# The skip product of a graph layer moved from the projection into the aggregation

## What is computed

```
for l in range(2):
    q, k, v = x @ Wq[l] + bq[l], x @ Wk[l] + bk[l], x @ Wv[l] + bv[l]   # 8 heads of 64
    a = (q[dst] * k[src]).sum(-1) * scale                              # scores, per edge and head
    alpha = softmax of a over the edges of each dst
    agg = segment_sum(alpha * v[src], dst)
    x = agg + (x @ Ws[l] + bs[l]) + enc                                # the skip product: x @ Ws[l]
```

## Time and profile before

| | us |
|---|---|
| median of 3 runs (3148.83 to 3156.06) | 3154.48 |
| the profiled execution | 3161.87 |
| its span, the time base of all rows | 3160.2 |

### The profile page before, as it was taken

One profiled execution on the slowest core, in us unless ns is written; L12 is line 12 of the kernel. 1 busy time (PEld: TensorE's weight loads), 2 busy tenths in 40 slices (PEclk: granted clock), 3 DMA queues, 4 the chain that ended last, 5 costly groups with the idle time before them and its releaser, 6 DMA issues. The chain is left out here.

```text
span 3160.2 us, 50179 instructions
## 1 busy us (share of the span) xinstructions
PE 2531.4 (80%) x9914; PEld 1849.9 (59%) x9914; DVE 2163.0 (68%) x3476; ACT 1170.8 (37%) x4350; POOL 1648.5 (52%) x1559
## 2 busy tenths in 40 slices
PE   1888787765898779977877669888785999699998
PEld 1666444443775557744544358666564767477776
DVE  5776677878977666657877888677464454566665
ACT  0554566654000021136666610001353322155554
POOL 0111677777777741146767777777122443355555
PEclk8999788986899989988888779999887999899999
DMA  2666777776777776667777767777432332251110
GB/s 96 237 239 213 246 240 242 240 236 197 204 218 220 218 236 228 197 216 238 240 242 239 221 185 214 213 224 221 150 134 93 106 121 93 98 167 41 40 46 33
DMA packets 244253, 575.14 MB, mean 182 GB/s; under 512 B 32642, under 2 KB 70894, under 8 KB 242834
## 3 DMA queue, kind: packets, MB, share of 16 engines
q0 software_dynamic: 100160, 328.28, 35.8%
q1 hardware_dynamic: 126546, 212.27, 19.7%
q10 hardware_dynamic: 17280, 31.63, 2.7%
HBM read 465.00 MB, written 107.06 MB: 181 GB/s over the span
## 5 line engine op out<-in xcount | busy, mean ns | idle before, releaser
L1357 POOL DMA_INDIRECT edge_ring<-k_rows,edges_src x626 | 592.7, 947 | 282.3 <-issue 135.9
L1357 POOL DMA_INDIRECT edge_ring<-v_rows,edges_src x626 | 617.2, 986 | 223.5 <-issue 140.6
L1666 PE MATMUL edge_psA<-layer_q_space 128*128 128x256 f32 (+1 forms) x2656 | 628.9, 392 | 95.3 <-DVE layer_q_space L1490 87.8
L1666 PEld LDWEIGHTS edge_psA<-layer_q_space 128*128 128x128 f32 x2656 | 495.5, 192 | 228.4 <-issue 159.2
L1490 DVE TENSOR_TENSOR layer_q_space<-edge_ring,edge_psQ 128x512 f32<-128x512 f32 x664 | 426.6, 683 | 162.1 <-SPq L1275 133.1
L1413 DVE TENSOR_TENSOR edge_ring<-edge_psQ,edge_ring 128x512 f32<-128x512 f32 x532 | 346.9, 682 | 175.5 <-ACT edge_ring L1502 71.6
L1502 ACT ACTIVATE edge_ring<-edge_ring 128x64 f32<-128x64 f32 x1328 | 320.1, 242 | 285.9 <-DVE edge_ring L1413 285.9
L1619 PE MATMUL edge_psQ<-layer_q_space,edge_hotT 128*128 x1064 | 363.3, 474 | 15.9 <-DVE edge_ring L1413 13.3
L108 PE MATMUL proj_psP<-proj_w,proj_xT 128*128 128x512 f32 x1440 | 354.9, 403 | 6.5 <-DVE proj_xT L866 4.0
L108 PEld LDWEIGHTS proj_psP<-proj_w,proj_xT 128*128 128x128 f32 x1440 | 270.8, 191 | 68.8 <-DVE proj_xT L866 4.4
L1394 DVE TENSOR_REDUCE layer_scores<-edge_ring 128x24 f32<-128x1536 f32 x166 | 289.1, 1742 | 0.0
(11 more groups left out here) (309 smaller groups left out, 3625.8 us busy)
## 6 DMA issues: line engine op xcount, KB each, us to landing
v_xT<-proj_xT SPq DMA_DIRECT2D x40, 512.0 KB, 4.9
edge_x_halves<-v_xT SPq DMA_DIRECT2D x80, 256.0 KB, 5.4
agg_rows<-layer_q_space ACTq DMA_DIRECT2D x40, 260.0 KB, 3.6
base_rows<-proj_enc SPq DMA_DIRECT2D x40, 256.0 KB, 2.0
k_rows<-proj_out ACTq DMA_DIRECT2D x40, 256.0 KB, 3.8
v_rows<-edge_ring ACTq DMA_DIRECT2D x40, 256.0 KB
edge_ring<-k_rows,edges_src POOLq DMA_INDIRECT x626, 4.0
edge_ring<-v_rows,edges_src POOLq DMA_INDIRECT x626, 3.8
```

The source lines that it names most:

```text
L1357: pool.indirect_dma_start(ring[:, buffer[n], :], None, rows, bass.IndirectOffsetOnAxis(ap=T["src"][:, t:t + 1], axis=0)).then_inc(landed[b ...
L1666: last = pe.matmul(psA[:, bass.ds(d % 2, 1), e, 0:hi - lo].rearrange("p o w -> p (o w)"), hot[:, s % R, :], wv[:, s % R, lo:hi], start=Fal ...
```

## The change

- **The skip product leaves the projection.** `normalise_project` and `combine_project` make K and Q alone (order K, Q, then S and V among the weights), 24 matmuls a tile. The residual that is stored has the skip bias but not the product. Half of the weights' parts are made before the first tile, the other half two at a time in tiles 0 to 3, and at tile 4 SP stores both V's and the skip's parts (2 MB each).
- **It comes back in the aggregation.** SP loads the skip's parts once, behind the masks, then the halves of x a second time, and the residual rows tile by tile. PE makes one chunk (three matmuls) at the start of a batch, four batches for a tile, from batch 2 on (`project_skip`). DVE adds the sum to the residual some batches later (`add_skip`), and SP stores it back.
- **Scores.** ACT makes the one-hots of a batch before it reduces the slot of two batches ago. GpSimd itself tells of landed gathers, four gathers later. SP keeps releases, rows and halves, sorted by slots.
- **First projection.** Four x buffers instead of three, the norm's statistics a tile ahead of its use, units sized and signed one by one, ACT's taking and DVE's rest ahead of DVE's Q addition, PE's unit transposes behind both products.

The core of the diff (`normalise_project` first; `combine_project` has the same edits for `range(2)`, `w_high`, `w_low`, `biased` and the two stores):

```diff
-        layer, XB = 0, 3
+        layer, XB = 0, 4
...
-        S_, K_, Q_, V_ = range(4)
+        K_, Q_, S_, V_ = range(4)
...
-                    if i == 1:
+                    if i == KC:
                         sp.wait_ge(w_lows, 4 * KC)
-                        sp.dma_start(later_v["w"].rearrange("p (h k c) -> p h k c", h=2, k=KC),
-                                     w[:, :, V_ * KC:(V_ + 1) * KC, :].bitcast(F32)).then_inc(v_parts_out, 16)
+                        for name, j in (("w", V_), ("skip_w", S_)):
+                            sp.dma_start(later_v[name].rearrange("p (h k c) -> p h k c", h=2, k=KC),
+                                         w[:, :, j * KC:(j + 1) * KC, :].bitcast(F32)).then_inc(v_parts_out, 16)
...
-                    sp.wait_ge(ready, i * 3 + S_ + 1)
+                    sp.wait_ge(biased, i + 1)
                     sp.dma_start(base_dram[i * P:(i + 1) * P, :], enc[:, i % 2, :]).then_inc(base_out[i % 2], 16)
...
-                    for j in range(3):
+                    for j in range(2):
...
                 for i in range(NT):
                     if i + 1 < NT:
                         high(i + 1)
+                    if i < KC:
+                        w_high(2 * KC + 2 * i)
+                        w_high(2 * KC + 2 * i + 1)
+                    for u in units(i):
+                        size(u)
+                        sign(u)
                     if i:
                         q_part(i - 1)
-                    if i + 2 < NT:
-                        ln.root(act, i + 2)
-                    for u in units(i):
-                        size(u)
                     for u in units(i - 1):
                         take(u)
-                    act.wait_ge(ready, i * 3 + K_ + 1)
+                    if i + 3 < NT:
+                        root(i + 3)
+                    act.wait_ge(ready, i * 2 + K_ + 1)
                     act.dma_start(k_dram[i * P:(i + 1) * P, :], out[:, i % 2, :]).then_inc(k_out[i % 2], 16)
-                    for u in units(i):
-                        sign(u)
...
                     if i + 2 < NT:
-                        normalise(i + 2)
-                    if i:
-                        q_less(i - 1)
-                    add(i, S_)
+                        apply(i + 2)
+                    if i + 3 < NT:
+                        stats(i + 3)
                     add(i, K_)
                     for u in units(i):
                         size_up(u)
-                    for u in units(i):
                         choose(u)
-                    add(i, Q_)
+                    if i:
+                        q_less(i - 1)
                     for u in units(i - 1):
                         low_unit(u)
+                    add(i, Q_)
```

In `edge_attention`, SP, GpSimd, DVE, ACT and PE in turn:

```diff
+                in_turn = [(r + 16, release, (r, multiplied)) for r in range(ET - 3)]
+                for k in range(2, -(-USED // PER_ROWS)):
+                    in_turn.append((k * PER_ROWS - 12, load_rows, (k,)))
+                for h in range(XH, 2 * NT):
+                    in_turn.append((done_in(h - XH) * B, load_half, (h,)))
+                for _slot, do, what in sorted(in_turn, key=lambda x: x[0]):
+                    do(*what)
                 sp.wait_ge(queried, USED)
                 sp.dma_start(masks, T["mask_rows"]).then_inc(masks_in, 16)
+                sp.dma_start(skip_rows[:, 1:, :], later_v["skip_w"].rearrange("p (n c) -> p n c", c=C)
+                             ).then_inc(skip_in, 16)
...
-                for t in range(ET):
-                    if t + AHEAD < ET:
-                        release(t + AHEAD - NV, weighted)
-                    arrive(ET + t, v_arrived)
+                in_turn = [(r + 10, release, (r, weighted)) for r in range(ET - NV)]
+                for h in range(XH, 2 * NT):
+                    i, half = divmod(h - XH, 2)
+                    in_turn.append(((S_AT[i] + 1 + 2 * half) * B, load_half, (2 * NT + h,)))
+                for i in range(NT):
+                    in_turn.append(((S_AT[i] + 7) * B + 1, store_base, (i,)))
+                    if i + 2 < NT:
+                        in_turn.append(((S_AT[i] + 9) * B, load_base, (i + 2,)))
...
+                def arrive(n):
+
+                    pool.wait_ge(*landing[n])
+                    pool.sem_inc(k_arrived if n < ET else v_arrived, 1)
...
                 for t in range(ET):
+                    if t >= FLIGHT:
+                        arrive(t - FLIGHT)
                     if t >= NB:
 
 
                         pool.wait_ge(k_released, t - NB + 1)
-                        pool.sem_inc(started, 1)
                     gather(t, k_dram, t)
...
+                def add_skip(i):
+                    vec.wait_ge(base_in[i % 2], i // 2 * 16 + 16)
+                    vec.wait_ge(s_projected, 4 * i + 4)
+                    vec.tensor_tensor(base_rows[:, i % 2, :], psS[i % 2], base_rows[:, i % 2, :], ALU.add
+                                      ).then_inc(s_added, 1)
...
-                    if j >= 2:
-                        reduce(j - 2)
                     act.wait_ge(spread, j + 1)
...
                     act.activation(hotT[j % 2], apart[:, j % 2, :], ACT.Relu, bias=1.0, scale=-1.0
                                    ).then_inc(hotT_ready, 1)
+                    if j >= 2:
+                        reduce(j - 2)
...
+                def project_skip(i, k):
...
+                    product(pe, psS[i % 2], [x_halves[:, h % XH, part, k % 2, :] for part in range(2)],
+                            [skip_row(part * KC + k) for part in range(2)], start=(k == 0), stop=(k == KC - 1)
+                            ).then_inc(s_projected, 1)
...
                 for s in range(USED):
+                    if s % B == 0 and s // B in s_steps:
+                        project_skip(*s_steps[s // B])
```

More of the change, by code:

```diff
@@ L775, in _ @@
                         for k in range(KC):
-                            last = product(pe, psP[(3 * i + j) % 4][:], [xT[:, i % 2, h, k, :] for h in range(2)],
+                            last = product(pe, psP[(2 * i + j) % 4][:], [xT[:, i % 2, h, k, :] for h in range(2)],
                                            [w[:, h, j * KC + k, :] for h in range(2)],
@@ L905, in _ @@
                                       ALU.subtract).then_inc(w_lows, 1)
+                for i in range(2 * KC):
+                    w_low(i)
                     if i == KC - 1:
@@ L1128, in _, with w_low @@
                 combine_tile(1)
-                for i in range(4 * KC):
+                def w_low(i):
                     vec.wait_ge(w_highs, i + 1)
```

226 lines of the change are left out of this document (138 added, 88 removed).

## The result

The changed kernel takes **3234.26 us** (median of 4 runs, 3233.13 to 3239.1) against 3153.72 for the kernel before on the same chip: a ratio of 1.026, with a 95% interval of 1.0243 to 1.0278. It is slower, by 81 us, where 85 us of gain had been forecast, and the time lies outside the range of 3020 to 3125.

The account below looks back on a forecast made before the run. GpSimd's gathers were taken to bound both edge stages, PE the second projection, unit work the first. Edges -7.5 a layer (-15 for two), projections -46 and -24: -85 us, to 3070 us; range 3020 to 3125.

Parts of the forecast that it names:

- Second projection: PE, near full there, loses 12 of 36 product matmuls a tile: gain of 46 us, bounds 35 to 54.
- First projection: Unit work, not PE, sets the pace; gain of 24 us, 6 in tiles with units and reload, bounds 0 to 45.
- The loop of 11.0 us a tile: First projection: ACT's unit work, SP's store and reload and the landing sum to 11.0 us a tile, against 11.3 before.
- The rival of a longer loop: First projection: the reload loop gets longer, gain -8 instead of -24, total 3086; chance 0.2.
- Scores, -15 a layer: K gathers: stalls and 18 us of release waits go, 3 given back to transfers; bounds -18 and 0.
- SP's release waits: GpSimd's waits read as SP's releases: 18 us in K, 9 in V a layer, both forecast to go.
- near 719: Scores: sign that the last K gather would start near 719 us, with PE's and GpSimd's named waits gone.
- Arrivals told by GpSimd four gathers later and a last store add 1.5: Aggregation: GpSimd's later telling of landed gathers, with a last store, costs 1.5 us a layer.
- must land within four issues, 5.0, so it has 1.2 in hand: Aggregation: a gather lands after 3.8 us and has 5.0, so a margin of 1.2 us.
- Added transfers, +12: Aggregation: added loads and stores slow gathers to a pace of 1.295 us, +12 a layer; bounds 0 to 45.
- The slower one: Aggregation: late gathers, four in flight, carry 1.55 us each, 80 a layer, total 3206; break-even pace 1.45; chance 0.06.
- the +3 forecast: Between scores and aggregation: SP's load of 2 MB skip weights costs V gathers 3 us a layer, 0 to 6.

## Why the prediction was wrong, point by point

- **Second projection: right.** 43.7 of 46. PE's products fell to 480, 24 a tile, and its share to 0.81 (128.41 of 158.00) with the DMA share at 0.83. By ACT's K stores a tile takes 6.1 us, where 6.3 was reckoned, but the one behind the weights' store takes 12.7; spreading that store gave another 4.6.
- **First projection: half right.** The loop of 11.0 us a tile came as reckoned. What was left out is the price of the 4 MB store *in that stage*: I had costed 2 MB at 5.9 us of DMA time in the second projection and between the stages, and not at the fifth tile of the first, where unit loads queue behind it. About 10 us, of which the spread stores gave 7.5 back; the other 6 us short of 24 stay open. The rival of a longer loop did not come about.
- **Scores, -15 a layer: the edits worked and the gathers did not get faster.** PE's waits for halves of x are gone, the last K multiplication starts 8.0 us after the last K gather (738.9, 730.9) instead of 24.2 after it (757.9, 733.7). But the 18 us that I read as SP's release waits were not to be had, nor the 9 in V: 16.7 of them in K and 8.7 in V were waits for landings, told by way of SP, and the landings of before alone, at four in flight, give 418 of the 419.9 us. With the wait back on the gather K gained 7; taking it off the gather turned that into a loss of 7.5 and 11.8. The sign "near 719" for the last K gather also left out the 24 us forecast for the first projection; with them it would be 695. It was 730.9.
- **The failing step stands in "Aggregation", in two sentences.** "Arrivals told by GpSimd four gathers later and a last store add 1.5": I priced the telling by when DVE hears of a row, not by what stands in GpSimd's queue between a landing and the next gather. That edit takes the landing wait off the gather, and it costs 12 to 13 in K and 10 to 12 in V on the kernel before, 15 to 19 and 24 to 25 in the changed one (the run with the wait on the gather): 77 of the 166 us between the 85 forecast as gain and the 81 measured as loss. And "must land within four issues, 5.0, so it has 1.2 in hand": a gather must land 0.26 us sooner than that before the change and 0.77 sooner after it, so there are 4.2 us for landings with a median of 3.9 to 4.3.
- **Added transfers, +12: too small, not wrong in kind.** With 0.77 us they cost 35 to 37 a layer. With 0.26 V is 28 longer than before (446.7 against 418.4); 19 of that lie behind the 90th gather, and there the transfers are what is left to explain them: without transfers the changed kernel paces those gathers like the kernel before with GpSimd telling, 1.34 us each. Two late edges in the same loop do not simply add; each takes margin from the other. The sentence on the Trainium skill ("DMA: Bandwidth & Descriptors", section "Queues, rings and completion order") worked out an estimate of 24 us a layer. The 19 lie between that and the 12 that I took from the scores' row, so they do not decide for either, and no run here shows the turns of packets.
- **Rivals.** The slower one named half of the mechanism, four in flight with landings too late, and the row that would show it, but not the wait taken off the gather; its pace of 1.55 us was too long (1.46 behind the first 15 gathers), its price of 80 a layer too high, and its 0.06 far too little. Its break-even pace of 1.45 was passed. K's part of the loss was in no rival.
- **What stays open.** The first 15 V gathers take 35.6 us instead of 18.8 in the changed kernel, and still 36.4 with the wait on the gather; part of this only moves a stall that came later before (the next 75 gathers took 1.48 us each before, 1.37 to 1.41 after). 8 to 9 us a layer of the 28 lie in these 90 gathers. The load of the skip weights is a small part of it: without that load, in the run with the skip kept in the projections, the first 15 still take 32.5 us (32.6 in the second layer, against 37.3), so it costs 3 to 5, close to the +3 forecast. Why the stall comes earlier I did not separate. Open too is why GpSimd takes half a microsecond more behind a semaphore instruction.

## What to carry to other kernels

Where an engine issues transfers with a fixed number in flight, the least time from a landing to the next issue belongs to the loop: work it out from the trace's landings, and price every instruction that a change puts between the two. Before calling a queue's wait the bound, put the trace's own landings through the rule of the loop; here that would have shown, without any new run, that four in flight already cost 25 us of each K pass and some 15 of each V pass (reckoned 418 and 409 at four, 393 and 393 at six), and that the cheapest change was the number itself. A wait that the profile puts down to another engine's signal should be held against the landings first, when that engine passes landings on. A change that moves transfers under such a loop should raise the number in flight first: here the same change lost 81 us with four and gained 37 to 40 with six.

## What the runs showed of the hardware that I had not expected

- On GpSimd's queue it matters where the wait for a landing stands. On the gather itself, the gather starts 0.26 us after the landing at the earliest; on a semaphore instruction ahead of the gather, 0.74 to 0.77 us after it, also for the first 28 K gathers of the changed kernel, which carry no other wait. That instruction's record is 17 ns long, and it appears in no row of busy time.
- More gathers in flight cost little in landing time here: from four to eight (the run with spread stores) the V gathers' median landing went from 4.3 to 4.8 us, while the DMA share of the aggregation rose from 0.77 to 0.87 and the rate from 236 to 280 GB/s.
- While a burst of 4 MB from SP's queue filled the DMA engines (a share of 1.01 from 133 to 150), transfers issued behind it landed late: a unit load that lands in 3.7 us as a rule (median of the line) took up to 9.7.
